# Third attention: scores from the raw context through one product of the query and key weights

## The chip, the cores and the metric

One core of a Trainium2 chip runs the whole program. The metric is the time of one execution on the device in microseconds (us). Three executions of the kernel before took 1595.96, 1596.53 and 1597.42 us, so the median is 1596.53.

## The reference, cut to what matters

The program is four gated blocks over x of shape (8, 128, 512), each an attention to the same context (8, 128, 512) and then a feed-forward network (FFN), always on a layer norm of x. The change concerns the third attention, which has one head of width 512:

```python
# text = _layernorm(x), features = ctx_4096, both (8, 128, 512); Wq, Wk (512, 512); bq, bk (512,)
Q = jnp.einsum('btx,dx->btd', text, Wq) + bq
K = jnp.einsum('bpx,dx->bpd', features, Wk) + bk
scores = jnp.einsum('btd,bpd->btp', Q, K) / sqrt(512)
attended = jnp.einsum('btp,bpd->btd', softmax(scores), features)
x = x + jnp.tanh(g_xattn[2]) * attended
```

The block before it is the FFN of the second block (a router over eight experts picks two, low-rank terms are added to a base product); the block after it is an FFN with a weight that is dequantised on the core, `(weight_q - zp) * scale`.

## The kernel before, in words

The program is written engine by engine: each engine has its own list of instructions, and semaphores (`wait_ge`, `then_inc`) are all that orders the engines against each other. From the first FFN on, the eight batches are taken in four pairs; `pairs_ahead` and `pairs_split` (helpers above the engine programs) run a body for pairs 0 to 3, and `pairs_split` puts an extra step between pair 1 and 2 (`third`), between 2 and 3 (`fourth`) and behind 3 (`end`). The stages have numbers: L1F is the second FFN, L2X the third attention, L2F the FFN behind it.

The large products are done in three passes (`PASSES`): each float32 operand is split in a high part (rounded by ScalarE, `high`) and a low part (the rest, by GpSimd's `rest` or by VectorE), and high x high, high x low and low x high are added up in PSUM. Smaller products take the float32 operands as they are; each is then two instructions in the trace. A layer norm is made one pair ahead: VectorE's `next_stats` (`ln_stats`) takes mean and variance of the next pair, GpSimd's `rsqrt` takes the root, `next_apply` (`ln_apply`) writes the rows `xn`, TensorE's `turn_next` transposes them into banks 0 and 1, ScalarE's `store_next` writes the high part `xnTp[0]` and VectorE's `next_lo` the low part `xnTp[1]`.

In L2X, per pair i, TensorE (`x2_pe`) transposes `xn` of pair i+1, makes the scores of pair i from `q2` and `k2` into banks 6 and 7 (L1624), the first three quarters of the keys of pair i+1 (`x2_keys`, L1448 through `split_product`) while the softmax runs, transposes the probabilities into banks 2 and 3 (L1632), makes the last quarter of the keys, then the output (L1638) into banks 6 and 7, then the queries of pair i+1 (`x2_queries`). VectorE (`x2_dve`) takes the row maxima (L2286), divides by the sums (L2290), makes the low part of the next x, statistics, the copy of the keys with their bias (L2280), the rows of the pair after, and at last adds the output into `x_res` (`update`, L2130), which frees banks 6 and 7; the scores of the next pair wait for it (`res`). Behind pair 0 VectorE also makes the offsets of the next FFN's weight (`f2_offsets`, L2543), behind pair 1 its scales (`f2_scales`, L2548); between ScalarE's pair 1 and 2 it rounds that weight (`f2_weights`), and GpSimd makes the low part. The context comes in a single buffer `cTp` by SyncE's DMA queue, and ScalarE and GpSimd split it (`context_high`, `context_rest`).

In L1F (`ffn_pe`, `ffn_dve`, `ffn_act`), TensorE makes router and low-rank products (L1459), the base product (L1472), transposes the weighted low-rank rows `hs` (L1477) once VectorE's routing chain has made them, transposes the next `xn` and adds the up product (L1481). ScalarE rounds the key and query weights between pair 1 and 2 (`x2_late`), and GpSimd makes their low parts behind pair 2's and pair 3's work.

Of the kernel before, what the change touches and what calls it, by code (L numbers as in the profile page):

```python
# [17 lines left out]
F32 = mybir.dt.float32  # L18
F32R = mybir.dt.float32r
# [92 lines left out]
def build(nc, A, out):  # L112
    with ExitStack() as ctx:
# [211 lines left out]
        wk2 = [sb(ctx_p, f"wk2_{l}", [P, DC, D], F32R) for l in range(2)]  # L325
        wq2 = [sb(ctx_p, f"wq2_{l}", [P, DC, D], F32R) for l in range(2)]
# [8 lines left out]
        w2 = [sb(ctx_p, f"w2_{l}", [P, DC, D], F32R) for l in range(2)]  # L335
        ctk = sb(ctx_p, "ctk", [P, 2, D])
        q2 = sb(ctx_p, "q2", [P, DC, PT2])
        k2 = sb(ctx_p, "k2", [P, DC, PT2])
# [29 lines left out]

        x_dram = A["x"].rearrange("b s d -> s b d")
# [32 lines left out]
        def _(sp):  # L402
# [123 lines left out]
            next_ctx(NPAIR + 1, 1)  # L526
            next_ctx(NPAIR + 2, 2)
            next_ctk(1)
            next_ctx(NPAIR + 3, 3)
# [8 lines left out]
            next_ctx(2 * NPAIR, 0)  # L538
            with sp.Fori(1, NPAIR) as i:
                next_ctx(2 * NPAIR + i, i)  # L540
# [8 lines left out]
        def _(pool):  # L549
# [137 lines left out]
            def x2_weights():  # L687
                pool.wait_ge(S("xn_ready"), NB * (L1F - 1) + NB)
                rest(wq2, raw2["q"], "wq2")
            pairs_split(pool, ffn_pool(L1F, tb["f1"]), nothing, x2_weights, x2_end)  # L690
            rsqrt(NPAIR * (L2X - 1) + 1)
            context_rest(NPAIR + 1)

            def x2_pool(i, last):
                if not last:
                    rsqrt(NPAIR * (L2X - 1) + i + 2)
                if not (isinstance(i, int) and i + 2 >= NPAIR):
                    context_rest(NPAIR + i + 2)
# [73 lines left out]
        def _(act):  # L772
# [163 lines left out]
            def ffn_act(L):  # L936
                second = int(L == L1F)

                def body(i, last):
                    for j in range(2):  # L940
                        act.wait_ge(S("ffn_top"), NB * second + 2 * i + j + 1)
                        act.activation(e2[:, j, :], m8[:, j, 0:1], ACT.Exp, bias=m8[:, j, 1:2], scale=-1.0)\
                           .then_inc(S("ffn_e2"), 1)
                    for j in range(2):
                        act.wait_ge(S("ffn_hst"), NB * second + 2 * i + j + 1)
                        act.activation(hsT[:, j, :], bank(2 + j)[:, 256:256 + P], ACT.Copy).then_inc(S("ffn_hsT"), 1)
                    store_next(L, i, last)
                return body

# [93 lines left out]
            def x2_queries(i):  # L1043
                for c in range(DC):
                    if c % 2 == 0:
                        act.wait_ge(S("q2_mm"), 2 * i + c // 2 + 1)
                    e = act.activation(q2[:, c, :], bank(2 + c // 2)[:, (c % 2) * PT2:(c % 2 + 1) * PT2], ACT.Identity,
                                       bias=bq2[:, c:c + 1], scale=float(D) ** -0.5)
                    if c % 2 == 1:
                        e.then_inc(S("q2_ready"), 1)  # L1050

            def x2_context(i):
                act.wait_ge(S("k2_mm"), 2 * i)
                context_high(NPAIR + i)

            def x2_act(i, last):
# [5 lines left out]
                for j in range(2):  # L1062
                    act.wait_ge(S("x2_tp"), 2 * i + j + 1)
                    act.activation(pT2[:, j, :], bank(2 + j)[:, 0:P], ACT.Copy).then_inc(S("x2_pT"), 1)
                if not (isinstance(i, int) and i + 2 >= NPAIR):
                    x2_context(i + 2)
# [87 lines left out]
            def x2_late():  # L1154
                act.wait_ge(S("wkq2_ld"), 64)
                for m, w in (("k", wk2), ("q", wq2)):
                    high(w[0], raw2[m][:], f"w{m}2")
            pairs_split(act, ffn_act(L1F), x2_late, nothing, lambda: context_high(NPAIR))
            act.wait_ge(S("scaled"), 1)
            x2_queries(0)  # L1160
            x2_context(1)

            def f2_weights():
                act.wait_ge(S("scaled"), 2)
                act.wait_ge(S("wq2_lo"), 1)
                act.wait_ge(S("wk2_lo"), 1)
# [32 lines left out]
        def _(pe):  # L1199
# [252 lines left out]
            def ffn_pe(L, f):  # L1452
                w, second = ffn[f], int(L == L1F)

                def body(i, last):
# [6 lines left out]
                    for j in range(2):  # L1462
# [4 lines left out]
                        for c in range(DC):  # L1467
# [5 lines left out]
                            else:  # L1473
                                pe.matmul(bank(4 + j), xnT[:, c, t], w["base"][:, c, :], start=c == 0, stop=False)  # L1474
                    for j in range(2):
                        pe.wait_ge(S("ffn_hs"), NB * second + 2 * i + j + 1)
                        pe.transpose(bank(2 + j)[:, 256:256 + P], hs[:, j, :], ident[:]).then_inc(S("ffn_hst"), 1)  # L1477
                    turn_next(L, i, last)
                    for j in range(2):
# [4 lines left out]
                pairs_ahead(pe, body)  # L1484
# [1189 lines left out]
```

## Time and profile before

| | |
|---|---|
| median of 3 executions | 1596.53 us |
| the profiled execution | 1596.18 us, its span 1594.5 us |
| TensorE busy | 98% of the span, 9066 products |
| VectorE, ScalarE, GpSimd busy | 62%, 50%, 30% |
| L1F and L2X together | about 1235 to 1350 us after the span's start |

The engines work side by side, so their shares don't add up. An engine's busy share says how much room it has on average; what bounds a stage is read from its own rows: who waits, how long, and for whom. Times of rows are microseconds from the span's start. A product's end is modelled in the profile, and products overlap: the duration of a merged row is a little longer than its part of the path, which the chain of waits gives.

### The profile page before, as it was taken

How to read it: one execution, taken by the hardware profiler on the slowest of the kernel's cores; microseconds unless marked ns; L12 is line 12 of the kernel's file. 1: busy time of each engine (PE TensorE's matmuls, PEld its weight loads, DVE VectorE, ACT ScalarE, POOL GpSimd, SP SyncE). 2: the span in 40 equal slices, each digit the busy share in tenths (PEclk: the TensorE clock that was granted, in tenths of full speed). 3: DMA queues.
4: the chain of work that ended last, by engine and by line, in shares of the span. 5: the costliest groups of instructions: out<-in, count | busy, mean ns of one | idle time of the engine just before them, and what ended most of it. 6: DMA issues, size and time to landing. Idle time of an engine off the chain costs nothing.

```text
span 1594.5 us, 26459 instructions
## 1 busy us (share of the span) xinstructions
PE 1556.7 (98%) x9066; PEld 1278.7 (80%) x9066; DVE 984.2 (62%) x2597; ACT 796.1 (50%) x2279; POOL 484.2 (30%) x350
## 2 busy tenths in 40 slices
PE   9999999999999999999999999999999999999987
PEld 7788888888888888888886888888898788766556
DVE  6762663635636446265476676767676767756677
ACT  5442443434424344244342476667677332288874
POOL 3131320312203213032112613232323543377651
PEclk9999999999999999999999999999999999999999
DMA  5110111101111111111234011020202613000001
GB/s 182 54 44 30 57 43 53 43 30 56 43 39 43 43 56 43 39 43 44 67 93 159 14 40 53 20 72 0 79 1 80 226 54 105 17 11 14 5 2 53
DMA packets 36597, 85.67 MB, mean 54 GB/s; under 512 B 5808, under 2 KB 18736, under 8 KB 34480
## 3 DMA queue, kind: packets, MB, share of 16 engines
q1 hardware_dynamic: 36528, 84.80, 16.2%
q8 instruction: 38, 0.62, 0.2%
q14 instruction: 31, 0.25, 0.1%
HBM read 82.69 MB, written 2.10 MB: 53 GB/s over the span
## 4 chain that ended last, share of the span: by engine, by line
PE 78%; DVE 9%; ACT 4%; issue 3%; DVEq 2%; POOL 1%; DMA 1%; POOLq 0%; SPq 0%; ACTq 0%
PE banks L1288 10%; PE banks L1233 10%; PE banks L1206 10%; PE banks L1214 10%; PE banks L1448 9%; PE banks L1561 4%; PE banks L1345 3%; PE banks L1328 3%; PE banks L1526 3%; PE banks L1335 2%; PE banks L1668 2%; PE banks L1675 1%; PE banks L1691 1%; PE banks L1474 1%; PE banks L1698 1%
## 5 line engine op out<-in xcount | busy, mean ns | idle before, releaser
L559 POOL TENSOR_TENSOR w_q<-w_raw_q,w_q 128x1792 fp32r<-128x1792 f32 x15 | 61.1, 4071 | 479.3 <-ACT w_q L796 479.3
L1288 PE MATMUL banks<-w_o,atT 128*128 128x512 f32 x720 | 181.0, 396 | 0.0
L1206 PE MATMUL banks<-cT,w_k 128*128 128x512 f32 x720 | 178.0, 396 | 0.0
L1233 PE MATMUL banks<-w_v,cT 128*128 128x512 f32 x768 | 176.6, 390 | 0.0
L1233 PEld LDWEIGHTS banks<-w_v,cT 128*128 128x128 f32 x768 | 143.9, 188 | 29.8
L1214 PE MATMUL banks<-xT,w_q 128*128 128x512 f32 x672 | 163.7, 394 | 0.7 <-ACT kT L786 0.7
L2004 DVE TENSOR_TENSOR sA<-banks,pbias 128x512 f32<-128x512 f32 x62 | 42.7, 690 | 186.6 <-PE banks L1328 185.8
L1206 PEld LDWEIGHTS banks<-cT,w_k 128*128 128x128 f32 x720 | 131.9, 188 | 25.5
L1288 PEld LDWEIGHTS banks<-w_o,atT 128*128 128x128 f32 x720 | 131.7, 188 | 25.6
L1214 PEld LDWEIGHTS banks<-xT,w_q 128*128 128x128 f32 x672 | 123.7, 188 | 26.1 <-ACT kT L786 1.2
L855 ACT ACTIVATE sA<-sA,nmA 128x128 f32<-128x128 f32 x248 | 96.4, 393 | 55.8 <-DVE nmA L2009 55.5
L786 ACT ACTIVATE vA<-banks 128x512 f32<-128x512 f32 x64 | 38.2, 597 | 134.2 <-PE banks L1233 134.2
L1448 PE MATMUL banks<-xnT_part,wq 128*128 128x256 f32 x768 | 101.1, 286 | 0.0
L2031 DVE TENSOR_TENSOR x_res<-banks,x_res 128x512 f32<-128x512 f32 x112 | 77.1, 688 | 35.8 <-PE banks L1288 34.7
L1448 PEld LDWEIGHTS banks<-xnT_part,wq 128*128 128x128 f32 x768 | 94.2, 190 | 2.2 <-issue 2.2
L1083 ACT ACTIVATE p<-banks,nm 128x128 f32<-128x128 f32 x256 | 91.8, 415 | 6.2 <-DVE nm L2364 6.0
L861 ACT ACTIVATE pTA<-banks 128x512 f32<-128x512 f32 x64 | 38.1, 595 | 105.4 <-PE banks L1335 105.3
L648 POOL TENSOR_TENSOR wo<-wo_raw,wo 128x512 fp32r<-128x512 f32 x48 | 60.9, 1303 | 82.6 <-ACT wo L985 82.6
L865 ACT ACTIVATE atT<-banks 128x512 fp32r<-128x512 f32 x62 | 37.1, 599 | 95.7 <-PE banks L1345 95.7
L971 ACT ACTIVATE p<-banks,nm 128x256 f32<-128x256 f32 x128 | 58.8, 482 | 47.8 <-DVE nm L2217 47.5
L2009 DVE CUSTOM_DVE_ANT_0 sA<-sA,madd 128x128 f32<-128x128 f32 x248 | 75.5, 359 | 8.4 <-issue 0.2
L729 POOL TENSOR_TENSOR p<-p,rs 128x512 f32<-128x512 f32 x64 | 67.2, 1056 | 41.0 <-DVE rs L2370 40.7
(298 smaller groups left out, 3403.4 us busy)
## 6 DMA issues: line engine op xcount, KB each, us to landing
wo_raw<-in_wo SPq DMA_DIRECT2D x16, 768.0 KB, 4.4
w_raw_v<-in_w0v SPq DMA_DIRECT2D x8, 1024.0 KB, 4.7
w_raw_q<-in_w0q SPq DMA_DIRECT2D x16, 512.0 KB, 3.3
w_raw_k<-in_w0k SPq DMA_DIRECT2D x15, 512.0 KB, 3.4
w_raw_o<-in_w0o SPq DMA_DIRECT2D x15, 512.0 KB, 3.3
cTp<-in_ctxT SPq DMA_DIRECT2D x12, 512.0 KB, 4.3
wq_raw<-in_wq SPq DMA_DIRECT2D x1, 3072.0 KB, 10.2
x_res<-in_x SPq DMA_DIRECT2D x4, 512.0 KB, 11.4
```

Source lines behind the costliest of these rows:

```text
L559: pool.tensor_tensor(w_part[slot][1][:], w_raw[slot][:], w_part[slot][0][:].bitcast(F32), ALU.subtract).then_inc(S(f"w{slot}_lo"), 1)
L729: pool.tensor_tensor(p3[:, U % 3, k], p3[:, U % 3, k], rs[:, U % 3, k].unsqueeze(2).to_broadcast([P, 4, P]), ALU.mult).then_inc(S(f"x3_p{h ...
L855: e = act.activation(s_at(p, g)[:, t, :], s_at(p, g)[:, t, :], ACT.Exp, bias=nmA[:, g % 2, t:t + 1], scale=-1.0, accum_out=smA[:, g % 2, t ...
L1083: e = act.activation(p3[:, U % 3, n, :], s[:, k, :], ACT.Exp, bias=nm[:, U % 3, n:n + 1], accum_out=sm[:, U % 3, n:n + 1])
L1206: mm = pe.matmul(dst, wk_[l][:, c, h * P:(h + 1) * P], cT[r][:, c, half * HT:(half + 1) * HT], start=c == 0 and n == 0, stop=c == DC - 1 a ...
L1214: mm = pe.matmul(dst, wq_[l][:, w, c, :], xT[r][:, x, c, :], start=c == 0 and n == 0, stop=c == 1 and n == len(PASSES) - 1)
L1233: mm = pe.matmul(dst, cT[l][:, c, b * P:(b + 1) * P], wv_[r][:, c, :], start=n == 0, stop=n == 3 * DC - 1)
L1288: mm = pe.matmul(dst, at_at(l, p, b // 4 * 2 + h)[:, t], w[r][:, h, :], start=start and n == 0, stop=stop and n == 5)
L1448: mm = pe.matmul(dst, w(l, c), x(r, c), start=c == 0 and n == 0, stop=c == DC - 1 and n == len(PASSES) - 1)
L1561: mm = pe.matmul(bank(6 + b), at1[l][:, NCH * k + c, b * P:(b + 1) * P], wo1[k][r][:, c, :], start=k == 0 and c == 0 and n == 0, stop=k == ...
L2009: e = dve.tensor_tensor_reduce(out=s_at(p, g)[:, t, :], in0=s_at(p, g)[:, t, :], in1=madd[:, 4 * half + t, :], scale=-1.0, scalar=0.1 * BI ...
L2031: dve.tensor_tensor(x_res[:, b, :], bank(6 + b % 2), x_res[:, b, :], ALU.add).then_inc(S("o_added"), 1)
```

## The change

The scores are rewritten: Q K^T = (xn Wq^T + bq)(ctx Wk^T + bk)^T. With M = Wq^T Wk, the product over features, it is xn M ctx^T, plus a term per context column (Wk^T bq, which is added to the new queries `q2` as their bias `u2`), plus terms per query row (xn Wq^T bk and bq bk), which cancel in the softmax; the kernel makes them all the same (`w2r`, `row_terms`), takes them off the negated maximum and adds them back, so that of them only a rounding is left. M is made once, in the last pair of L1F; its 4 quarters are split into high and low part by ScalarE and VectorE. The key projection, the copy of the keys and the splits of the context for this stage are gone; the scores read the context as it is loaded, from two buffers in turn (`cTp`, `cTb`). The queries of the next pair take the place of the next keys, beside the softmax, and nothing stands between the output and the next transposes. `next_lo` moves to the front of VectorE's list of a pair, `row_terms` (one product and sum per row tile) is added to it, and each row maximum is followed by two small operations with drains. The weights are rounded one pair earlier each. The new FFN weight `w2` now lies where the query weights lay.

```diff
@@ the DMA queue (SyncE)
+            def next_ctx2(i):
+                sp.wait_ge(S("cT_ld"), 16 * (NPAIR + i))
+                if i > 1:
+                    sp.wait_ge(S("x2_s"), 2 * (i - 1))
+                sp.dma_start(ctx2(i)[:], A["ctxT"][:, :, i * PT2:(i + 1) * PT2]).then_inc(S("cT_ld"), 16)
...
@@ GpSimd
-            def x2_end():
-                pool.wait_ge(S("xn_ready"), NB * (L1F - 1) + NB + 2)
-                rest(wk2, raw2["k"], "wk2")
-                context_rest(NPAIR)
...
+            def x2_weights(m, w, n):
+                pool.wait_ge(S("xn_ready"), NB * (L1F - 1) + n)
+                rest(w, raw2[m], f"w{m}2")
+            pairs_split(pool, ffn_pool(L1F, tb["f1"]), lambda: x2_weights("k", wk2, NB - 2),
+                        lambda: x2_weights("q", wq2, NB), nothing)
...
@@ ScalarE
+            def weights_high(c):
+                act.wait_ge(S("m2_mm"), c + 2)
+                act.activation(m2[0][:, c, :], bank(6 + c % 2), ACT.Copy).then_inc(S("m2_hi"), 1)
...
-            def x2_context(i):
-                act.wait_ge(S("k2_mm"), 2 * i)
-                context_high(NPAIR + i)
...
@@ TensorE, L1F, last pair
+                    if last and second:
+                        x2_weights(0)
                     for j in range(2):
                         pe.wait_ge(S("ffn_hs"), NB * second + 2 * i + j + 1)
                         pe.transpose(bank(2 + j)[:, 256:256 + P], hs[:, j, :], ident[:]).then_inc(S("ffn_hst"), 1)
+                    if last and second:
+                        x2_weights(1)
                     turn_next(L, i, last)
+                    if last and second:
+                        x2_weights(2)
+                        x2_weights(3)
...
-                pairs_ahead(pe, body)
+                pairs_split(pe, body, nothing, x2_biases if second else nothing, nothing)
+
+            def x2_biases():
+                pe.wait_ge(S("wkq2_ld"), 64)
+                for c in range(DC):
+                    pe.matmul(bank(6), bk2[:, c:c + 1].to_broadcast([P, P]), raw2["q"][:, c, :], start=c == 0, stop=c == DC - 1)
+                for d in range(DC + 1):
+                    for c in range(DC):
+                        w = raw2["k"][:, c, d * P:(d + 1) * P] if d < DC else bk2[:, c:c + 1].to_broadcast([P, P])
+                        mm = pe.matmul(bank(7)[:, d:d + 1], w, bq2[:, c:c + 1], start=c == 0, stop=c == DC - 1)
+                mm.then_inc(S("m2_mm"), 1)
+
+            def x2_weights(c):
+                if c == 0:
+                    pe.wait_ge(S("wk2_lo"), 1)
+                    pe.wait_ge(S("wq2_lo"), 1)
+                    pe.wait_ge(S("scaled"), 1)
+                if c > 1:
+                    pe.wait_ge(S("m2_lo"), c - 1)
+                for o in range(DC):
+                    for n, (l, r) in enumerate(PASSES):
+                        mm = pe.matmul(bank(6 + c % 2), wq2[l][:, o, c * P:(c + 1) * P], wk2[r][:, o, :],
+                                       start=o == 0 and n == 0, stop=o == DC - 1 and n == len(PASSES) - 1)
+                mm.then_inc(S("m2_mm"), 1)
...
@@ TensorE, L2X
             def x2_pe(i, last):
                 turn_next(L2X, i, last)
-                pe.wait_ge(S("k2_ready"), 4 * i + 4)
+                pe.wait_ge(S("cT_ld"), 16 * (NPAIR + i + 1))
                 pe.wait_ge(S("res"), NB * L2X + 2 * i)
...
-                            mm = pe.matmul(bank(6 + j)[:, 0:P], q2[:, c, j * P:(j + 1) * P], k2[:, c, j * P:(j + 1) * P],
+                            mm = pe.matmul(bank(6 + j)[:, 0:P], q2[:, c, j * P:(j + 1) * P], ctx2(i)[:, c, j * P:(j + 1) * P],
...
-                    x2_keys(i + 1, range(DC - 1))
+                    x2_queries(i + 1, range(DC - 1))
                 for j in range(2):
                     pe.wait_ge(S("x2_p"), 2 * i + j + 1)
-                    pe.transpose(bank(2 + j)[:, 0:P], p2[:, j, :], ident[:]).then_inc(S("x2_tp"), 1)
+                    pe.transpose(bank(4 + j)[:, 0:P], p2[:, j, :], ident[:]).then_inc(S("x2_tp"), 1)
                 if not last:
-                    x2_keys(i + 1, (DC - 1,))
+                    x2_queries(i + 1, (DC - 1,))
...
-                if not last:
-                    x2_queries(i + 1)
...
@@ VectorE, L1F: store_biases stands between pair 2 and 3; in the last pair, behind next_apply:
+                        row_terms(0)
+                        weights_low(0)
+                        weights_low(1)
...
                     next_lo(L, i, last)
+                        weights_low(2)
+                        weights_low(3)
...
+            def store_biases():
+                dve.wait_ge(S("m2_mm"), 1)
+                dve.tensor_scalar(u2[:], bank(7)[:, 0:DC + 1], float(D) ** -0.5, None, ALU.mult)
+                dve.tensor_scalar(w2r[:], bank(6), float(D) ** -0.5, None, ALU.mult).then_inc(S("scaled"), 1)
+
+            def row_terms(i):
+                dve.drain()
+                for j in range(2):
+                    dve.tensor_tensor_reduce(out=xw2[:], in0=xn[:, j, :], in1=w2r[:], scale=1.0, scalar=0.0, op0=ALU.mult,
+                                             op1=ALU.add, accum_out=r2[:, i % 2, j:j + 1])
+                    dve.drain()
...
@@ VectorE, L2X
             def x2_dve(i, last):
+                next_lo(L2X, i, last)
                 for j in range(2):
                     dve.wait_ge(S("x2_s"), 2 * i + j + 1)
-                    dve.tensor_reduce(nm[:, j, 0:1], bank(6 + j)[:, 0:P], AX_X, ALU.max, negate=True).then_inc(S("x2_max"), 1)
+                    dve.tensor_reduce(nm[:, j, 0:1], bank(6 + j)[:, 0:P], AX_X, ALU.max, negate=True)
+                    dve.drain()
+
+                    dve.scalar_tensor_tensor(out=nm2[:, j], in0=nm[:, j, 0:1], scalar=u2[:, DC:DC + 1],
+                                             in1=r2[:, i % 2, j:j + 1], op0=ALU.subtract, op1=ALU.subtract)
+                    dve.drain()
+                    dve.scalar_tensor_tensor(out=nm[:, j, 0:1], in0=nm2[:, j], scalar=u2[:, DC:DC + 1],
+                                             in1=r2[:, i % 2, j:j + 1], op0=ALU.add, op1=ALU.add).then_inc(S("x2_max"), 1)
...
-                next_lo(L2X, i, last)
                 if not last:
                     next_stats(i + 1)
-                    x2_keys(i + 1)
                     next_apply(L2X, i + 1)
+                    if i + 2 < NPAIR:
+                        row_terms(i + 2)
```

The host hands over Wq and Wk untransposed instead of transposed, in the same sizes.

## Rows read from the trace of the kernel before

**Rows 1.** The page: busy time (share of the span), and one group of weight loads.

```profile
PE 1556.7 (98%) x9066; PEld 1278.7 (80%) x9066; DVE 984.2 (62%) x2597; ACT 796.1 (50%) x2279; POOL 484.2 (30%) x350
...
L1448 PEld LDWEIGHTS banks<-xnT_part,wq 128*128 128x128 f32 x768 | 94.2, 190 | 2.2 <-issue 2.2
```

**Rows 2.** TensorE in order of time: start, duration, line, tiles, count, wait before.

```profile
1244.56 0.53 PE L1477 MATMUL banks<-ident,hs 128*128 128x128 f32 x2 [2.11 <-DVE hs L2164]
...
1270.53 2.02 PE L1459 MATMUL banks<-f1ra,xnT 128*128 128x136 f32 x16
...
1279.26 0.53 PE L1477 MATMUL banks<-ident,hs 128*128 128x128 f32 x2 [1.21 <-DVE hs L2164]
...
1295.44 2.05 PE L1624 MATMUL banks<-k,q 128*128 128x128 f32 x16 [0.27 <-DVE k L2280]
...
1312.33 1.95 PE L1624 MATMUL banks<-k,q 128*128 128x128 f32 x16
...
1328.25 1.95 PE L1624 MATMUL banks<-k,q 128*128 128x128 f32 x16
...
1344.16 1.95 PE L1624 MATMUL banks<-k,q 128*128 128x128 f32 x16
```

**Rows 3.** The chain of waits: start, time on the path, engine, line, count.

```profile
1249.70 1.85 PE banks L1459 x16
1251.55 5.51 PE banks L1472 x24
...
1257.28 0.87 PE banks L1428 x8
1258.15 1.73 PE banks L1481 x4
...
1312.50 1.79 PE banks L1624 x16
...
1321.88 5.67 PE banks L1448 x48
```

**Rows 4.** VectorE in order of time, columns as in rows 2.

```profile
1289.18 1.00 DVE L1992 TENSOR_SCALAR xn<-x_res,mv,rstd 128x512 f32<-128x512 f32 x2 [0.90 <-POOL rstd L595]
...
1313.88 0.29 DVE L2286 TENSOR_REDUCE nm<-banks 128x1 f32<-128x128 f32 x1 [3.09 <-PE banks L1624]
...
1314.69 0.17 DVE L2181 RECIPROCAL rs<-sm 128x1 f32<-128x1 f32 x1
1314.93 0.29 DVE L2290 TENSOR_SCALAR p<-p,rs 128x128 f32<-128x128 f32 x1
...
1315.58 1.28 DVE L2122 TENSOR_TENSOR xnT_part<-banks,xnT_part 128x512 fp32r<-128x512 f32 x2
1316.78 1.28 DVE L1980 BATCH_NORM_STATS2 stat<-x_res 128x6 f32<-128x512 f32 x2
...
1318.46 0.17 DVE L1985 TENSOR_SCALAR ve<-mv 128x2 f32<-128x2 f32 x1
...
1322.35 1.40 DVE L2130 SCALAR_TENSOR_TENSOR x_res<-banks,gates,x_res 128x512 f32<-128x512 f32 x2
...
1331.81 1.10 DVE L2290 TENSOR_SCALAR p<-p,rs 128x128 f32<-128x128 f32 x1
```

**Rows 5.** VectorE: a line's durations (ns min/median/max), and a group (count, busy us, mean ns).

```profile
L2543 DVE TENSOR_TENSOR zp<-w2q,zp x4: 677/678/1220, 1307.8 to 1310.1; 128x512 f32<-128x512 int32 x4
...
L2009 DVE CUSTOM_DVE_ANT_0 sA<-sA,madd 128x128 f32<-128x128 f32 x248 | 75.5, 359 | 8.4 <-issue 0.2
```

**Rows 6.** ScalarE and GpSimd in order of time, columns as in rows 2.

```profile
1328.30 1.91 ACT L927 ACTIVATE w<-zp 128x2048 fp32r<-128x2048 f32 x1
...
1330.29 5.03 POOL L617 TENSOR_TENSOR w<-zp,w 128x512 fp32r<-128x512 f32 x4 [5.85 <-ACT w L927]
```

**Rows 7.** TensorE by stretches: length, busy (count), granted clock, DMA share, GB/s.

```profile
1244.00:1250.00 6.00, 5.32 (x19) 0.72 0.96 362
1278.00:1284.00 6.00, 4.66 (x26) 1.00 0.00 0
```

More of the change, by code:

```diff
@@ L325, in build @@
         wk2 = [sb(ctx_p, f"wk2_{l}", [P, DC, D], F32R) for l in range(2)]
+        ctx_x = ExitStack()
+        w2 = [sb(ctx_x, f"w2_{l}", [P, DC, D], F32R) for l in range(2)]
+        ctx_x.close()
         wq2 = [sb(ctx_p, f"wq2_{l}", [P, DC, D], F32R) for l in range(2)]
@@ L334, in build @@
         ctx_x.close()
-        w2 = [sb(ctx_p, f"w2_{l}", [P, DC, D], F32R) for l in range(2)]
+        m2 = [sb(ctx_p, f"m2_{l}", [P, DC, D], F32R) for l in range(2)]
         ctk = sb(ctx_p, "ctk", [P, 2, D])
         q2 = sb(ctx_p, "q2", [P, DC, PT2])
-        k2 = sb(ctx_p, "k2", [P, DC, PT2])
+        cTb = sb(ctx_p, "cTb", [P, DC, PT2])
+        u2 = sb(ctx_p, "u2", [P, DC + 1])
+        w2r = sb(ctx_p, "w2r", [P, D])
+        xw2 = sb(ctx_p, "xw2", [P, D])
+        r2 = sb(ctx_p, "r2", [P, 2, 2])
+        nm2 = sb(ctx_p, "nm2", [P, 2, 1])
         p2 = sb(ctx_p, "p2", [P, 2, P])
@@ L1063, in x2_act @@
                     act.wait_ge(S("x2_tp"), 2 * i + j + 1)
-                    act.activation(pT2[:, j, :], bank(2 + j)[:, 0:P], ACT.Copy).then_inc(S("x2_pT"), 1)
-                if not (isinstance(i, int) and i + 2 >= NPAIR):
-                    x2_context(i + 2)
+                    act.activation(pT2[:, j, :], bank(4 + j)[:, 0:P], ACT.Copy).then_inc(S("x2_pT"), 1)
                 if not last:
@@ L1474, in body @@
                                 pe.matmul(bank(4 + j), xnT[:, c, t], w["base"][:, c, :], start=c == 0, stop=False)
+                    if last and second:
+                        x2_weights(0)
                     for j in range(2):
@@ L1477, in body @@
                         pe.transpose(bank(2 + j)[:, 256:256 + P], hs[:, j, :], ident[:]).then_inc(S("ffn_hst"), 1)
+                    if last and second:
+                        x2_weights(1)
                     turn_next(L, i, last)
+                    if last and second:
+                        x2_weights(2)
+                        x2_weights(3)
                     for j in range(2):
@@ L1827, in _ @@
             ffn_pe(L1F, "f1")
-            pe.wait_ge(S("wq2_lo"), 1)
+            pe.wait_ge(S("m2_lo"), DC)
             x2_queries(0)
-            pe.wait_ge(S("wk2_lo"), 1)
-            pe.wait_ge(S("res"), NB * L2X)
-            x2_keys(0, range(DC))
-            pairs_ahead(pe, x2_pe)
+            for i in range(NPAIR):
+                x2_pe(i, i == NPAIR - 1)
             pe.wait_ge(S("wf_lo"), DC + 1)
@@ L2168, in body @@
                     next_apply(L, i)
+                    if last and second:
+                        row_terms(0)
+                        weights_low(0)
+                        weights_low(1)
                     if last and L == L0F:
@@ L2173, in body @@
                     next_lo(L, i, last)
+                    if last and second:
+                        weights_low(2)
+                        weights_low(3)
                     for j in range(2):
@@ L2552, in _ @@
             next_apply(L2X, 0)
[L2553 removed]
+            row_terms(1)
             x2_dve(0, False)
```

67 lines of the change are left out of this document (29 added, 38 removed).

## The prediction

> **What bounds the kernel now.** I read the page first: TensorE is busy for 98% of the span [rows 1], so what counts is TensorE's own order and its waits. The change touches two stages, the last pair of the second FFN and the third attention. I read TensorE's timeline there: where blocks follow one another without a bracket, TensorE is the bound, and a bracket names whom it waited for [rows 2]. There are few: 1.21 us for VectorE's routing chain in the last FFN pair, 2.11 us for the same chain in the first. The scores of the four pairs start at 1295.44, 1312.33, 1328.25 and 1344.16: periods of 16.9, 15.9 and 15.9 us. The chain of waits gives what each block costs on the path, without the pipeline's overlap [rows 3]. I read VectorE, ScalarE and GpSimd as well [rows 4 to 6], because a period will lose a third of its TensorE work, and it has to be seen what then ends last.
>
> I count from E, the end of a pair's scores. Now E0 is 1297.2 (1295.44 + 1.79) and E3 is 1345.95: 48.7 us apart.
>
> **Up to E0: the weight product is made.** From the start of the last FFN pair (1270.53 [rows 2]) to E0 there are 26.7 us now.
>
> Added on TensorE, first (a) the bias terms. Four float32 products with 512 columns are eight instructions; four such take 1.73 us [rows 3], so 3.5 us. Then 20 float32 products with one column, 40 instructions. No row has one column. The nearest are float32 blocks of 128 columns, 8 in 0.87 us, 0.109 each [rows 3]; they load 128x128 weights each time too, and I take it that the load sets the pace: 40 x 0.109 = 4.4 us. Lower end: half of it, 2.2, if it was the columns that cost 0.109. Upper end: 0.19 each, a load from start to end with nothing beside it [rows 1], 7.6. So (a) is 7.9 us, between 5.7 and 11.1. The Trainium skill (TensorE: Matmul & The Clock Gate, LDWEIGHTS) says that a load takes one cycle of 1.2 GHz per column, 107 ns for 128; no row here shows a load that sets the pace; by it the 40 would take 4.3 us. Then (b) the product M, 4 x 12 products with 512 columns: 24 take 5.51 us [rows 3], so 11.0 us.
>
> Removed up to E0: the first pair's keys, 48 products with 256 columns, 5.67 us (as the queries [rows 3]), 1.21 us of waiting that M covers, and the waits for the context's low part and the keys, 1 to 2 us.
>
> The new order on TensorE: biases 7.9, router 1.85, base 5.5, M 11.0, transposes 0.22 and 0.87, up 1.73, queries 5.67, transposes 0.87, scores 1.79: 37.4 us. Is TensorE late anywhere in it? VectorE now waits for the biases ahead of its statistics, so the routing result comes about 4.5 us after the router's products; the base product (5.5) and the first quarter of M (2.75) cover that. A quarter of M is split by ScalarE (0.6, a quarter of the 1.9 for 2048 columns and its start [rows 6]) and VectorE (0.68, as one low part, 1.28 for two [rows 4]) in 1.5 us with the hops; 3.7 us of other work stand between quarters 1 and 3, and 1.73 us (up) behind the last: covered by 0.2. The splits of the two weights move earlier on ScalarE and GpSimd, one to each pair, into time in which both wait. E0 comes 37.4 - 26.7 = **10.7 us later**.
>
> **E0 to E3.** Per pair TensorE loses the keys and keeps queries 5.67, transposes 1.09, scores 1.79, output 1.73: 10.3 us. Were this the period, 17.8 us would come back. Two things speak against it. The scores of pair i+1 go to banks 6 and 7, which hold the output of pair i until VectorE has added it: now the queries (5.67) stand between and hide that, after it only a block of transposes (0.87). And VectorE's low part of the next x, which the queries need, stands behind everything VectorE did for the pair before, the offsets and scales too. So VectorE's list becomes the path:
>
> The first reduction can start 0.4 us before E, as now (1313.88 against 1314.3), or behind the low parts (1.28). Both softmaxes now end 1.75 us after it (1315.6 [rows 4]); four small operations at 0.24 each (start to start, 1314.69 to 1314.93) make it 2.7. Statistics to variance 1.85 (1316.78 to 1318.63). GpSimd's root 0.9 of waiting, as at 1289.18: the keys that stood there are gone. Rows of x 1.0. The row terms, two products summed over 512 elements: the nearest row is that operation on 128 elements, 0.359; 384 more at 1.17 ns (0.6 for 512 in the two-input rows, which show 0.678 with 0.08 of overlap [rows 5]) give 0.8, less the overlap, so 1.6 for both with drains; between 1.2 and 2.2. Updates 1.4. ScalarE's copies and exponentials lie inside the waits named.
>
> Pair 0: the low parts end at E+0.1; softmax to 2.8; variance 4.7; root 5.6; rows 6.6; row terms 8.2; updates 9.6; scores 1.8. TensorE is through with the output and transposes at 8.7. Period **11.4**.
>
> Pair 1: ahead of it VectorE does the offsets, 4 x 0.6 = 2.5 us (the one of 1.22 lay on GpSimd's context split, which goes [rows 5]). They start with the scores, end at E+0.65, the low parts at 2.0: TensorE's queries wait 2.0 us. Softmax 4.7, variance 6.5, rows 8.4, row terms 10.1, updates 11.5, scores: **13.3**.
>
> Pair 2: the scales, 2.5 us, end at E+0.8. ScalarE waits for them and rounds the FFN weight (1.9 us [rows 6]) ahead of its copies of the transposed x (two of 512 columns, 1.0): low parts at 4.4, and TensorE stands still until then. GpSimd's split of that weight (5.0 us [rows 6]) now lies on the softmax: a multiplication that takes 0.29 took 1.10 beside it [rows 4]. Softmax to 8.6, variance 10.4, rows 12.3, no row terms, updates 13.7, scores: **15.5**. By the Trainium skill (GPSIMD Engine Reference, Specifications) GpSimd also contends with VectorE instructions that read two inputs from SBUF, as the new small ones do. The trace agrees with the stretched first offset (1.22 against 0.678); by it pair 2 would be some 0.7 us longer.
>
> The clock: behind the wait of 2.11 us the granted clock went to its lower level, 1.2 GHz, for a time, 0.72 on average over 6 us, so 1.7 us lost; behind 1.21 us nothing was lost [rows 2, 7]. The waits of 2.0 and 4.4 us may do the same to the queries behind them. In pair 1 VectorE's list hides most of it and the fall is even odds: +0.3. In pair 2 the output comes later than VectorE: +0.8.
>
> The periods: 11.4 + 13.6 + 16.3 = 41.3 against 48.7, **7.4 us back**; the hops between engines that I counted at nothing, 0.15 a period, take 0.5.
>
> **Behind E3** nothing covers the last softmax: the small operations put its second half back by 0.8 us, 0.1 of which the order of the halves takes up: **+0.7**. The context's DMAs move earlier (two buffers, read in place) and cost nothing.
>
> **Sum.** 10.7 - 7.4 + 0.5 + 0.7 = +4.5 us on the profiled execution's 1596.18 (span 1594.5 and 1.7 around it): 1600.7. It lies 0.35 below the median of the runs, 1596.53, so **1601.0**. What a measurement can tell from no change is about 0.2%, 3.2 us.
>
> **Rivals.**
> *TensorE keeps the bound* (not slower): the wait for the updates ahead of the scores is short, and offsets and scales find room. Period 10.3 to 10.8, so 10.7 - 17 + 0.7 = -5.6: **1591**. For it: VectorE is busy for only 62% of the span [rows 1], and the offsets and scales cost nothing now. Against: it decides from the point where VectorE's list is below 10.3 us, and I count 11.4 without the offsets. 0.19.
> *The small terms are small*: one-column products at half the price (-2.2), no fall of the clock (-1.1): +1.2 us, or up to +3: **1598.5**. For it: the fall was seen behind 2.11 us only. 0.25.
> *All of it costs*: 40 one-column products leave the array nearly empty for over 4 us, the clock falls behind them and router and base lose 1.7; one-column products at 0.13 (+0.8), GpSimd stretches the small operations (+0.7), the clock costs full price twice (+1.5): **1605.5**. No row has such a stretch. 0.12.
> *My forecast*, +3.3 to +6.5 us (1599.8 to 1603): 0.44.
>
> The range, 1592 to 1605, leaves out most of the first rival and the upper part of the third. Slower 0.44 + 0.12 less what touches the bound, 0.55; the same 0.26; faster 0.19.
>
> **What would show it.** In the changed profile: the biases near 7.9 us and the first scores near 1306 on TensorE; brackets ahead of the scores that name VectorE's update, and ahead of queries that name the low part, the longest in the last pair's; periods growing from 11.4 to 16 us though the TensorE work in them is equal; a granted clock below full behind those waits. I am wrong if the periods are equal and near 10.3 us, if the one-column products cost under 2 or over 8 us, or if time is won or lost outside 1270 to 1350.

## The result, and the profile after

The changed kernel takes 1608.68 us (median of 4 executions, 1606.17 to 1611.11) against 1596.97 for the kernel before on the same chip (4 executions, 1595.96 to 1597.76): a ratio of 1.0077, interval 1.0065 to 1.009. It is slower by 12 us; the prediction was slower by 4.5, and 1608.68 lies above its range. The profiled executions are 1607.45 and 1596.18 us, their spans 11.0 us apart.

The page of the kernel after, against [rows 1]: TensorE has 96 products fewer and is busy 4.5 us longer.

```profile
PE 1561.2 (97%) x8970; PEld 1279.1 (80%) x8970; DVE 984.7 (61%) x2618; ACT 794.4 (49%) x2279; POOL 471.7 (29%) x334
```

TensorE of the kernel after in order of time (start, duration, line, tiles, count, wait before), the lines that answer to [rows 2]:

```profile
1272.28 3.60 PE L1514 MATMUL banks<-wq_raw,bk 128*128 128x512 f32 x8
1275.71 3.63 PE L1518 MATMUL banks<-bq,wk_raw 128*128 128x1 f32 x32
1279.20 1.03 PE L1518 MATMUL banks<-bq,bk 128*128 128x1 f32 x8
1280.10 3.59 PE L1476 MATMUL banks<-f1ra,xnT 128*128 128x136 f32 x16
1283.33 6.03 PE L1489 MATMUL banks<-f1base,xnT_part 128*128 128x512 f32 x24
1289.19 2.91 PE L1531 MATMUL banks<-wk,wq 128*128 128x512 f32 x12
...
1309.56 1.95 PE L1669 MATMUL banks<-cTp,q 128*128 128x128 f32 x16
...
1320.98 2.02 PE L1669 MATMUL banks<-cTb,q 128*128 128x128 f32 x16 [0.61 <-issue]
1324.53 4.54 PE L1465 MATMUL banks<-xnT_part,m 128*128 128x256 f32 x36 [1.53 <-DVE xnT_part L2163]
...
1333.92 2.02 PE L1669 MATMUL banks<-cTp,q 128*128 128x128 f32 x16 [0.61 <-issue]
1340.25 6.80 PE L1465 MATMUL banks<-xnT_part,m 128*128 128x256 f32 x36 [4.30 <-DVE xnT_part L2163]
...
1351.29 2.02 PE L1669 MATMUL banks<-cTb,q 128*128 128x128 f32 x16
1356.21 1.09 PE L1677 MATMUL banks<-ident,p 128*128 128x128 f32 x2 [2.89 <-DVE p L2356]
1357.14 3.75 PE L1683 MATMUL banks<-ctk,pT 128*128 128x512 f32 x4
1360.03 4.38 PE L1465 MATMUL banks<-w,xnT_part 128*128 128x512 f32 x12
```

The reader is to see four things. The block of biases stands at 1272.28 to 1280.10. The three blocks of queries carry brackets that grow, 0, 1.53 and 4.30 us. The same 36 instructions take 4.54 us and then 6.80, and the router's 16 take 3.59 where they took 2.02 [rows 2]. And the last softmax leaves a wait of 2.89 us, with a slow output block (3.75 against 1.96 at full clock) behind it.

TensorE by stretches of the kernel after (length, busy, count, granted clock, DMA share, GB/s), against [rows 7]:

```profile
42.00:44.00 2.00, 2.00 (x12) 0.50 0.00 0
...
1278.00:1280.00 2.00, 2.00 (x21) 1.00 0.00 0
1280.00:1282.00 2.00, 2.00 (x13) 0.63 0.00 0
1282.00:1284.00 2.00, 2.00 (x10) 0.52 0.00 0
1284.00:1286.00 2.00, 2.00 (x11) 1.00 0.00 0
...
1342.00:1344.00 2.00, 2.00 (x11) 0.50 0.00 0
...
1358.00:1360.00 2.00, 2.00 (x4) 0.50 1.09 353
```

Of the kernel before, two stretches were below full clock, that of [rows 7] and the last microseconds of the program. The kernel after has both and four more: behind the one-column products, behind the waits of 4.30 and 2.89 us, and one at 40 to 46 us, behind a wait of 2.1 us in a stage that the change doesn't touch. That wait is in the kernel before too, and its profile shows no fall there; of the 13 profiles of changed kernels 7 have it. I take it for chance. One profile of the kernel before can't show how frequent it is there, but its other executions show that falls come and go in it too: its fastest, 1592.32 us, has a mean granted clock of 1.0, and one of 1597.99 us has 0.996. Each fall is to 0.50, 1.2 GHz.

Where the 11.0 us are, before and after, by starts of blocks on TensorE:

| stretch | before | after | difference | predicted |
|---|---|---|---|---|
| up to the last FFN pair (a clock fall at 40 us) | 1270.53 | 1272.28 | +1.8 | 0 |
| from there to the first scores | 24.91 | 37.28 | +12.4 | +10.7 |
| first to last scores | 48.72 | 41.73 | -7.0 | -6.9 |
| last scores to the next FFN's first product | 5.67 | 8.74 | +3.1 | +0.7 |
| behind that | 244.7 | 245.5 | +0.8 | 0 |

VectorE of the kernel after, columns as in [rows 4]: its wait for the biases, the update ahead of the second scores, and its work around the last two pairs:

```profile
1280.27 0.17 DVE L2230 TENSOR_SCALAR u<-banks 128x5 f32<-128x5 f32 x1 [5.87 <-PE banks L1518]
...
1319.47 1.41 DVE L2171 SCALAR_TENSOR_TENSOR x_res<-banks,gates,x_res 128x512 f32<-128x512 f32 x2
...
1338.90 1.29 DVE L2163 TENSOR_TENSOR xnT_part<-banks,xnT_part 128x512 fp32r<-128x512 f32 x2 [2.49 <-ACT xnT_part L936]
1340.11 0.28 DVE L2345 TENSOR_REDUCE nm<-banks 128x1 f32<-128x128 f32 x1
1340.46 0.51 DVE L2348 SCALAR_TENSOR_TENSOR nm<-nm,u,r 128x1 f32<-128x1 f32 x1
1341.05 1.18 DVE L2351 SCALAR_TENSOR_TENSOR nm<-nm,u,r 128x1 f32<-128x1 f32 x1
...
1342.51 0.97 DVE L2348 SCALAR_TENSOR_TENSOR nm<-nm,u,r 128x1 f32<-128x1 f32 x1
...
1351.11 1.28 DVE L2021 BATCH_NORM_STATS2 stat<-x_res 128x6 f32<-128x512 f32 x2
...
1352.78 0.17 DVE L2026 TENSOR_SCALAR ve<-mv 128x2 f32<-128x2 f32 x1
1352.86 1.28 DVE L2163 TENSOR_TENSOR xnT_part<-banks,xnT_part 128x512 fp32r<-128x512 f32 x2
1354.06 0.28 DVE L2345 TENSOR_REDUCE nm<-banks 128x1 f32<-128x128 f32 x1
```

The last pair's first reduction stands behind the statistics for the next FFN (1351.11 to 1352.95) and the low parts. TensorE's scores had begun at 1351.29. In late_stats, below, where the statistics stand elsewhere, the reduction starts 1.62 us behind the start of the scores; here that would be 1352.91, and it starts at 1354.06, 1.15 us later. The bracket of 0.61 us ahead of the scores at 1320.98 names no engine, but the update that frees their banks ends at 1320.88.

### The profile page after: what moved, and what is told of

The parts are those of the page before. It is cut to its first block, busy times and chain, and to the rows that moved or that the text cites. A ratio compares the mean times of both kernels' runs of the same rounds, so it can differ in the third digit from the quotient of the medians.

```text
span 1605.5 us, 26211 instructions
## 1 busy us (share of the span) xinstructions
PE 1561.2 (97%) x8970; PEld 1279.1 (80%) x8970; DVE 984.7 (61%) x2618; ACT 794.4 (49%) x2279; POOL 471.7 (29%) x334
## 4 chain that ended last, share of the span: by engine, by line
PE 77%; DVE 8%; issue 5%; ACT 4%; DVEq 2%; POOL 1%; DMA 1%; SPq 0%; POOLq 0%; ACTq 0%
PE banks L1305 10%; PE banks L1250 10%; PE banks L1223 10%; PE banks L1231 9%; PE banks L1465 8%; PE banks L1610 4%; PE banks L1362 3%; PE banks L1345 3%; PE banks L1575 3%; PE banks L1352 2%; PE banks L1711 2%; PE banks L1718 1%; PE banks L1734 1%; PE banks L1491 1%; PE banks L1741 1%
## 5 line engine op out<-in xcount | busy, mean ns | idle before, releaser
L1465 PE MATMUL banks<-xnT_part,wq 128*128 128x256 f32 x576 | 76.7, 286 | 0.0
L2067 DVE TENSOR_TENSOR atT<-banks,atT 128x512 fp32r<-128x512 f32 x62 | 42.9, 692 | 52.0 <-ACT atT L877 51.9
## 6 DMA issues: line engine op xcount, KB each, us to landing
x_res<-in_x SPq DMA_DIRECT2D x4, 512.0 KB, 11.3
```

What stands on the lines that cost most here:

```text
L1465: mm = pe.matmul(dst, w(l, c), x(r, c), start=c == 0 and n == 0, stop=c == DC - 1 and n == len(PASSES) - 1)
```

## The experiments

All kernels but the last four are the changed kernel with one edit. They were timed in three sets, each beside the kernel before, whose median was 1596.23 us in the first set (after_again to early_dequant in the table), 1595.63 in the second (one_pass_m, fill_waits, other_banks, all_four) and 1595.82 in the third. A difference between medians of two sets carries what the sets differ by, up to 0.6 us for the kernel before. The gains below are differences of medians to after_again; by the ratios, those of one_pass_m, fill_waits and no_row_terms are 7.8, 3.2 and 7.3 us. Medians and ratios to the kernel before:

| kernel | us | ratio, interval |
|---|---|---|
| after_again | 1608.31 | 1.0076, 1.0063 to 1.0089 |
| wide_bias | 1604.32 | 1.0050, 1.0037 to 1.0063 |
| late_stats | 1605.13 | 1.0062, 1.0049 to 1.0075 |
| early_dequant | 1599.85 | 1.0024, 1.0013 to 1.0035 |
| one_pass_m | 1599.69 | 1.0027, 1.0016 to 1.0038 |
| fill_waits | 1604.81 | 1.0056, 1.0042 to 1.0070 |
| other_banks | 1607.82 | 1.0075, 1.0060 to 1.0091 |
| no_row_terms | 1599.89 | 1.0030, 1.0018 to 1.0042 |
| all_four | 1594.36 | 0.9988, 0.9979 to 0.9997 |
| three_no_banks | 1594.53 | 0.9992, 0.9983 to 1.0001 |
| all_no_rows | 1589.02 | 0.9961, 0.9948 to 0.9974 |
| all_no_rows_fill | 1588.92 | 0.9955, 0.9942 to 0.9968 |

**The changed kernel again (after_again).** Nothing is edited.

> The changed kernel once more, beside the others. Both theories: some 11 us above the kernel before (1607 to 1609). The theory of the clock (T1: part of the added time is TensorE at 1.2 GHz behind waits and behind the one-column products) expects its times to scatter by 2 us and more, since a wait of 2.1 us near 42 us and others near 1246 and 1338 may or may not be followed by a fall; the theory of work and waits alone (T2) expects them as close together as those of the kernel before.

The loss repeats. The scatter, on which the two theories differ, decides nothing: the five executions lie within 2.0 us, but the 13 of the kernel before beside them within 4.5. The falls behind the biases, the 4.30 and the 2.89 us wait are there again; that at 40 us is not, another stands at 1268, behind a wait of 1.59 us. TensorE shows the clock going down within the one-column block itself:

```profile
1274.85 3.69 PE L1518 MATMUL banks<-bq,wk_raw 128*128 128x1 f32 x32
1278.39 1.85 PE L1518 MATMUL banks<-bq,bk 128*128 128x1 f32 x8
1280.10 3.98 PE L1476 MATMUL banks<-f1ra,xnT 128*128 128x136 f32 x16
```

**Bias products with 96 equal columns (wide_bias).**

```diff
-mm = pe.matmul(bank(7)[:, d:d + 1], w, bq2[:, c:c + 1], ...)
+mm = pe.matmul(bank(7)[:, d * 96:(d + 1) * 96], w, bq2[:, c:c + 1].to_broadcast([P, 96]), ...)
```

> The 20 one-column bias products get 96 equal columns each (the bias column repeated), one of which is used; the loads are the same. T1: the products keep their 4.4 us, because the load of 128x128 sets the pace, but the array is filled, the granted clock stays full behind them, and router and base products get back their 1.7 us: 1.5 to 2 us below the changed kernel. T2 (the clock fell there by chance, or the columns cost): no change, or 0 to 2 us slower.

The copy `u2` takes one column of each 96. It is 4.0 us faster than the changed kernel, more than expected. TensorE:

```profile
1276.18 3.71 PE L1518 MATMUL banks<-bq,wk_raw 128*128 128x96 f32 x32
1279.73 1.06 PE L1518 MATMUL banks<-bq,bk 128*128 128x96 f32 x8
1280.62 2.05 PE L1476 MATMUL banks<-f1ra,xnT 128*128 128x136 f32 x16
```

Ninety-six times the columns cost next to nothing: all the biases take 7.87 us against 7.82. So the columns don't set the pace, 0.109 us each. What is left is the load of the 128x128 float32 weights; no run varies the load by itself. An estimate from the rule of the Trainium skill (TensorE: Matmul & The Clock Gate, LDWEIGHTS) is 107 ns for 128 columns; at full clock the runs agree, but the last eight of after_again, at the lower clock, took 0.21 us each. And behind the wider products the router takes 2.05 us and not 3.59: the clock stays up.

One pair of profiles could be chance, but all of them agree: in each of the eight with one-column products the clock falls within or behind that block, in each of the five with 96 columns (this one and the last four of the table) it stays full there. From the end of the biases to M it is 7.39 us instead of 9.09, 1.7 won in the profile; in after_again it was 9.86 us. The rest of the 4.0 us isn't the biases': between the profiles of after_again and wide_bias, 4.1 us apart in span, 3.3 us are won from the biases to the first scores, and 2.2 behind them, where the same two waits are followed by shorter falls (the queries take 6.05 us and not 7.01); 1.4 are lost ahead of the biases.

**The next FFN's statistics behind the last softmax (late_stats).**

```diff
-                if i == NPAIR - 2:
-                    next_stats(0)
...
+                if last:
+                    next_stats(0)
```

> VectorE's statistics for the FFN behind (1.8 us), which the move of the low parts to the front put ahead of the last pair's softmax, go behind that softmax. T1: the last softmax starts 1.3 us earlier, TensorE waits 1.6 instead of 2.9 us for it, and the clock no longer falls there: 3 to 4 us below the changed kernel. T2 (the wait counts, the clock does not): 1.3 us below. If the statistics were hidden: 0.

As expected, 3.2 us, though two of its six executions, at 1607.9 us, lie within the range of the changed kernel (1607.0 to 1609.0). TensorE behind the last scores (1351.82):

```profile
1355.60 0.33 PE L1677 MATMUL banks<-ident,p 128*128 128x128 f32 x1 [1.75 <-DVE p L2356]
...
1356.38 1.96 PE L1683 MATMUL banks<-ctk,pT 128*128 128x512 f32 x4
1358.62 3.04 PE L1465 MATMUL banks<-w,xnT_part 128*128 128x512 f32 x12 [0.29 <-DVE x_res L2171]
```

The wait is 1.75 instead of 2.89 us and here no fall follows it. From the scores to the next FFN 6.80 us, where it was 8.74; the FFN block another 1.3 us less. So 1.1 of the +3.1 us is what the prediction meant by +0.7, and the rest is the statistics (the wait is 1.14 us shorter) and the clock. That the clock holds is not certain: three_no_banks, below, has the same wait and a fall.

**Offsets and scales of the FFN weight while VectorE waits for the biases (early_dequant).**

```diff
             def store_biases():
+                f2_offsets()
+                f2_scales()
...
-            f2_offsets()
             x2_dve(1, False)
-            f2_scales()
...
```

> The offsets and scales of the next FFN's weight (2.5 us each on VectorE) move from behind pair 0 and 1 of the third attention into VectorE's wait for the bias products (5.9 us). T1: TensorE's waits for the low parts (1.5 and 4.3 us) go, and with the second one the fall of the clock behind it; periods 11.4, 11.4 and about 12 instead of 11.4, 12.9 and 17.4: 6.5 to 7.5 us below the changed kernel. Rival (the periods are long for the updates of the output and the row terms, the offsets lie beside them): 0 to 2 us below.

It wins 8.5 us, a little more than expected. TensorE's scores now come 11.41, 11.15 and 11.46 us apart, with the brackets on the low part gone:

```profile
1308.63 1.95 PE L1669 MATMUL banks<-cTp,q 128*128 128x128 f32 x16
...
1320.04 2.02 PE L1669 MATMUL banks<-cTb,q 128*128 128x128 f32 x16 [0.62 <-issue]
1321.82 4.52 PE L1465 MATMUL banks<-xnT_part,m 128*128 128x256 f32 x36
...
1331.19 2.02 PE L1669 MATMUL banks<-cTp,q 128*128 128x128 f32 x16 [0.61 <-issue]
1332.97 4.56 PE L1465 MATMUL banks<-xnT_part,m 128*128 128x256 f32 x36
...
1342.65 2.02 PE L1669 MATMUL banks<-cTb,q 128*128 128x128 f32 x16 [0.60 <-issue]
```

Eight operations of VectorE, 5 us of work that cost nothing in the kernel before, cost 7.7 us of the periods in the changed one (1.4 of them by the clock, as fill_waits shows), and nothing again where VectorE waited 5.87 us for the biases. They don't fit into that wait, though. There they take 8.2 us, since the offsets, with GpSimd at work beside them until 1275.1, take 5.63 us instead of 2.49, and VectorE takes up the biases 2 us late (1280.09; TensorE is through with them at about 1278). In this kernel TensorE has enough to do until then.

**M from the high parts alone (one_pass_m).**

```diff
-                    for n, (l, r) in enumerate(PASSES):
-                        mm = pe.matmul(bank(6 + c % 2), wq2[l][:, o, c * P:(c + 1) * P], wk2[r][:, o, :], ...)
+                    mm = pe.matmul(bank(6 + c % 2), wq2[0][:, o, c * P:(c + 1) * P], wk2[0][:, o, :], ...)
```

> The weight product M is made with the high parts alone, one pass of three (the low-order two thirds of the product are left out; the splits, waits and copies stay). 32 of 48 products with 512 columns go, 7.3 us. T1 (M lies on TensorE's path from end to end): 7 to 7.5 us below the changed kernel, 1601. Rival (VectorE's routing chain and the splits would end last anyway, M fills waits): 2 to 5 us below.

From the biases to the first scores it takes 30.01 us (1272.93 to 1302.94) instead of 37.28: 7.3 less for 32 products taken out, 0.23 each. M lies wholly on the path. The median fell by 8.6, by the ratios 7.8; the profile explains 7.3.

**Idle products in the waits of pair 2 and the last pair (fill_waits).** 16 and 11 products of the identity with itself, into a free bank, behind the scores.

```diff
+                for k in range({NPAIR - 2: 16, NPAIR - 1: 11}.get(i, 0)):
+                    pe.matmul(bank(4)[:, 0:P], ident[:], ident[:], start=True, stop=True)
```

> The same kernel with 16 idle products of 128 columns (3.5 us) ahead of the queries that wait 4.3 us in the third pair, and 11 (2.4 us) in the last pair's wait of 2.9 us; nothing reads them. T1: the clock stays full behind both waits, and output, queries and the first product of the next FFN get back what they lose: 3 to 4 us below the changed kernel. T2 (the fall costs nothing, since VectorE's list ends last): 0, or slower by the fillers' overhang.

As expected, 3.5 us, for work that computes nothing:

```profile
1336.69 3.74 PE L1674 MATMUL banks<-ident 128*128 128x128 f32 x32
1341.15 4.55 PE L1465 MATMUL banks<-xnT_part,m 128*128 128x256 f32 x36 [0.73 <-DVE xnT_part L2165]
...
1356.49 1.95 PE L1685 MATMUL banks<-ctk,pT 128*128 128x512 f32 x4
1358.43 3.05 PE L1465 MATMUL banks<-w,xnT_part 128*128 128x512 f32 x12
```

The queries begin as late as before and take 4.55 us instead of 6.80. So the slow blocks were slow by the clock, and the clock fell by the emptiness ahead of them. The last period is 15.95 us instead of 17.37; the prediction had 15.5 for it without a fall.

**The output in other banks (other_banks).** Then the scores needn't wait for the update; the wait moves to the transposes of the probabilities, behind the queries.

```diff
-                pe.wait_ge(S("res"), NB * L2X + 2 * i)
...
                     x2_queries(i + 1, range(DC - 1))
+                pe.wait_ge(S("res"), NB * L2X + 2 * i)
...
-pe.matmul(bank(6 + j), pT2[:, j, :], ctk...
+pe.matmul(bank(4 + j), pT2[:, j, :], ctk...
```

> The output of a pair goes to banks 4 and 5, so the scores of the next pair no longer wait for VectorE's update (the wait moves to the transposes of the probabilities). T1: only pair 0 gains its 0.6 to 0.8 us, since in the pairs behind it VectorE's list, with offsets or scales and the low parts, ends last all the same: 0 to 1 us below the changed kernel. Rival (the wait of the scores for the update is what lengthens the periods, as the prediction has it first): 2 to 4 us below.

No gain that can be told. Scores at 1310.02, 1320.67, 1335.13 and 1352.28: the first period is 0.8 us shorter, and the next wait for the low part takes it back (2.38 instead of 1.53 us, and a fall of the clock behind it). The bank was a wait in sight, not the bound.

**Without the row terms (no_row_terms).** The terms that cancel in the softmax, their products, `w2r`, `row_terms` and the two small operations behind each maximum are left out.

```diff
-pe.matmul(bank(6), bk2[:, c:c + 1].to_broadcast([P, P]), raw2["q"][:, c, :], ...)
...
-row_terms(i + 2)
```

> The changed kernel without the terms per query row, which cancel in the softmax: no product for w2r (3.5 us), no bq bk (0.9 us), no row_terms on VectorE (1.6 us a pair), no small operations behind the maxima (1.0 us a pair). The sum is the same in exact arithmetic. T1: 4.3 us less up to the first scores, 1 us in pair 0 where VectorE's list ends last, 1 in pair 2 and behind the last pair together, less chance of the clock falling behind 3.5 us of one-column products: 6 to 9 us below the changed kernel (1599 to 1602). Rival (the row terms and small operations lie beside TensorE's work): 4.3 us alone.

8.4 us less. In the profile 4.4 of them lie ahead of the first scores (32.88 us), 1.9 in the periods (10.82, 12.35, 16.62), and 1.9 behind the last scores (6.88), where the wait is 2.13 us and in this profile no fall follows it. One-column products remain, and so does the fall behind them.

**The four repairs together (all_four).** wide_bias, late_stats, early_dequant and other_banks.

> Wide bias products, late statistics, early offsets and scales, and the output in banks 4 and 5, together. T1: the sum of the parts with the bank change now worth some 0.7 a pair, periods near 10.5 us each and no fall of the clock: 8.5 + 4 + 3 + 1.5 less some overlap, 14 to 17 us below the changed kernel, 1592 to 1595, so 2 to 4 us below the kernel before. Rival (the parts overlap, and a TensorE period of 10.3 us is not reached since VectorE's list is 9.5 us and more): 10 to 12 below, no better than the kernel before.

14 us less than the changed kernel, at the lower end, and 1.3 below the kernel before (1.9 by the ratio), within what I called no change. Periods 10.63, 10.54 and 10.97: TensorE is the bound of the stage again, but for one wait of 0.21 us. Single gains were 4.0, 3.2, 8.5 and 0.5, together 16.2; a part is won only once. The last wait is 2.06 us, and a fall is back behind it.

**The same without the other banks (three_no_banks).**

> All four parts but the bank change: wide bias products, late statistics, early offsets and scales. T1: once offsets and scales no longer end last, each of three periods pays the scores' wait for VectorE's update, 11.4 against 10.6: 2 to 3 us above the run with all four (1594.4). Rival (the bank change is worth as little as alone): within 0.5 us of it.

A miss: 1594.53 against 1594.36. The profile does show what I expected in the periods (11.41, 11.15, 11.47, 1.9 us more in all), but 0.9 is given back behind the last scores (6.80 us against 7.67), where the wait is 1.75 instead of 2.06. The profiled executions are 1.3 us apart, the medians 0.2; both are less than the runs of one kernel scatter (1592.0 to 1598.6), so what the banks are worth beside the other three stays open. A fall of the clock stands behind the wait of 1.75 us:

```profile
1346.35 0.33 PE L1677 MATMUL banks<-ident,p 128*128 128x128 f32 x1 [1.75 <-DVE p L2358]
...
1347.13 2.85 PE L1683 MATMUL banks<-ctk,pT 128*128 128x512 f32 x4
```

**All of it, without the row terms (all_no_rows).**

> All four parts, and no row terms. T1: 4.3 us of bias products go from TensorE's path, VectorE's list gets 2.6 us shorter, which TensorE's 10.3 us periods hide, and the last softmax ends 0.8 us earlier: 5 to 6 us below the run with all four (1594.4), so 1588 to 1590, below the kernel before by 6 to 8. Rival (something else, the DMAs of the context copy or the routing, ends last as soon as TensorE is lighter): 2 to 3 below it.

1589.02 us, 6.8 below the kernel before (6.2 by the ratio). Its profile has a mean granted clock of 1.0, and TensorE goes through the stage thus:

```profile
1286.55 0.53 PE L1496 MATMUL banks<-ident,hs 128*128 128x128 f32 x2 [1.80 <-DVE hs L2203]
...
1304.30 1.95 PE L1666 MATMUL banks<-cTp,q 128*128 128x128 f32 x16
...
1336.00 1.95 PE L1666 MATMUL banks<-cTb,q 128*128 128x128 f32 x16
1339.08 0.68 PE L1675 MATMUL banks<-ident,p 128*128 128x128 f32 x2 [1.13 <-DVE p L2347]
```

From the last FFN pair (1270.90) to the first scores 33.4 us, then 31.7, then 5.84 to the next FFN: 70.9 against 79.3 in the kernel before. This is what the rewriting is worth once VectorE's list is short. The first line shows what is still lost: the shorter block of biases (3.55 us) leaves VectorE later still with the offsets and scales, which end only at 1281.2, and TensorE waits 1.80 us for the routing result in the midst of M. Early offsets and scales aren't free here; no run tries another place for them.

**With six idle products in its last wait (all_no_rows_fill).** The loop of fill_waits, in the last pair alone and into another free bank.

> The same with 6 idle products (1.3 us) in the last pair's wait for its softmax. T1: the wait there is some 1.5 us by now and the clock falls behind it only at times: 0 to 1.5 us below the run without them. Rival: no change.

1588.92 us, no change: behind the wait of 1.13 us that all_no_rows has there, its profile shows no fall to take away. It and all_no_rows are the fastest versions, and beat both kernels.

## Why the prediction was wrong

**Right: the mechanism and the periods.** VectorE's list became the path behind the first scores. I had periods of 11.4, 13.6 and 16.3 us and 0.5 for hops, 41.8; measured 11.42, 12.94 and 17.37, 41.73. The waits that I named are there: for the low part, 1.53 us (predicted 2.0) and 4.30 (4.4), and for the update 0.61 us ahead of two of the four scores, which other_banks takes away. early_dequant shows the cause: without the offsets and scales in the periods all three are 11.3 on average.

**Right: the biases.** "So (a) is 7.9 us": it is 7.82, and wide_bias shows that the columns don't set the pace.

**Failed: the clock behind the one-column products.** The prediction's sum has nothing for it: it put "No row has such a stretch" against it and left it to the rival of 0.12, whose 1.7 us are what the profile shows. It is 1.7 us of the +12.4; the 10.7 was otherwise right. Twenty products with one moving column, 4.4 us of them, let the clock go down as a wait does; 96 columns at the same pace do not.

**Failed: "Behind E3 ... +0.7".** The prediction's sum left out VectorE's statistics for the next FFN. It was +3.1, and 0.8 more behind it. I counted the small operations and did not read VectorE's program up to the end of pair 2: `next_stats(0)` stood there before, harmless, for the low parts came after the softmax. The change moves the low parts to the front of the list, and the statistics with them ahead of the last reduction. late_stats takes 3.2 us off. The statistics put the reduction back by 1.15 us. The wait becomes 2.89 us, a fall of the clock follows, and the slow blocks behind it cost more than the statistics: 3.75 and 4.38 us, where fill_waits has 1.95 and 3.05 without the fall, 2.3 us from start to start.

**Mis-sized, and luck: pair 2.** I had +0.8 for the clock; by fill_waits it is 1.4 (a period of 15.95 against 17.37). The contention with GpSimd hit other operations than those in the sum. "Softmax to 8.6" holds 1.5 us for the two multiplications that were stretched in [rows 4]; now they start behind GpSimd's split and take 0.29 us each. Instead the small operations took 0.51, 1.18 and 0.97 us for 0.22, in all 0.29 + 0.96 + 0.75 = 2.0. The Trainium skill (GPSIMD Engine Reference, Specifications) names that contention, the trace agrees with it, and I had it as 0.7 in a sentence beside the sum. So a wrong term of 1.5 stood in for a missing one of 2.0. And a pair 1 without a fall, 0.8 shorter than I had it, made up for what pair 2 had too little, so the right sum of the periods is partly luck.

So of the 6.5 us between my +4.5 and the +11.0 of the profiles, 1.7 are the clock behind the biases, 3.2 the last softmax with its wait and its fall, and 1.8 the fall at 40 us, which is no effect of the change that I can show. The median of the runs is another 1.2 us above the profiled execution.

**The rivals.** "TensorE keeps the bound" was false in the changed kernel, and is what all_four and all_no_rows bring about: periods of 10.4 to 11.0 us, where it had 10.3 to 10.8. "All of it costs", 1605.5 (its terms add up to 1605.7), was the nearest: its clock behind the one-column products came true, its one-column products at 0.13 us didn't.

## What to carry to other kernels

When TensorE loses work in a loop, write out the next engine's whole list for one turn, what other stages have put in its gaps included, and what stands at its ends when something is moved to the front: here 5 us of free side work became 7.7 us of path, and a place in a wait made it free again, as long as TensorE had other work behind that wait. Count an empty or nearly empty TensorE twice, once for the wait and once for the slow block behind it. Terms that cancel are not free either: leaving them out won 7 to 8 us in one kernel and 4 to 5 in another.

## What the runs showed of the hardware

- A wait costs more than its length. In these stages all 13 waits of TensorE of 2.89 us and more were followed by a granted clock of 0.50, and the queries behind those of 4.30 us took 6.05 to 7.01 us for 4.54. Behind the eight waits of 1.53 or 1.54 us it never fell. Between them it went either way: it fell behind 1.59 us (after_again), 1.75 (three_no_banks), 2.06 (all_four) and 2.38 (other_banks), and not behind 1.55 (three_no_banks), 1.57 and 1.80 (all_no_rows), 1.75 (late_stats) and 2.13 (no_row_terms). Of the twelve profiles that wait 2.09 to 2.15 us for the first routing result, eleven show a fall there, all_no_rows doesn't. What decides stays open. The Trainium skill (TensorE: Matmul & The Clock Gate, Part 1) says that the number of slow products varies between runs of one kernel; the runs agree, and here whether there are any does too.
- A TensorE that is 100% busy by the profile can lose its clock: 40 instructions of one column, back to back, went from 0.111 us each (3.54 for 32, start to start) to 0.21 for the last eight (1.71, after_again), and all eight profiles with such a block show a fall in it or behind it, none of the five with 96 columns.
- Two-input operations of VectorE on one element per partition took up to 1.38 us (early_dequant; 1.18 in the kernel after), six times their 0.22, beside GpSimd's split of the FFN weight.
